# A state-space scan with a routed convolution: delta, B and C from one product, B and C spread by transfers, TensorE's work placed anew over the slots

## The chip, the cores and the metric

The kernel runs on one core of a Trainium2 chip. A core has five engines with instruction queues of their own, each in order: TensorE (PE, matmuls into PSUM), VectorE (DVE), ScalarE (ACT), GpSimd (POOL) and SyncE (SP, which here only issues DMAs); ACT issues DMAs too. Engines wait for each other through semaphores. The metric is the device time of one execution in microseconds (us), lower is better.

## The reference

Sixteen images of 48 channels, 64x64, float32, taken as two layer-norm blocks with a residual each. Block 0 ends in a feed-forward net, block 1 in another; between them stands a Mamba scan over the low frequencies of a 2-D DCT. What is computed, cut to what matters:

```python
# per image: 48 x 64 x 64, fp32
x = x + ffn0(LN(x))
w = softmax(router(LN(x)))             # a choice of experts per image
y = conv1x1(gelu(sum_e w[e] * dwconv3x3(LN(x), e)))   # routed 3x3 depthwise convolution
f = dct2(x * similarity_mask(x))       # 64 x 64 -> four quadrants q of 32 x 32, L = 1024 steps
for q in range(4):
    xi, z = in_proj[q](f[q])           # 96 channels each
    xi = silu(conv1d(xi))              # taps folded into the input product here
    dt, B, C = xp[q](xi)               # B and C: 16 states (NS) each
    delta = softplus(dt_w[q] @ dt + bias)
    h[d, n, t] = exp(delta[d, t] * A[d, n]) * h[d, n, t-1] + delta[d, t] * xi[d, t] * B[n, t]
    yq = (sum_n C[n, t] * h[d, n, t] + D[d] * xi[d, t]) * silu(z)
    f[q] = out_proj[q](yq)
x = x + y + idct2(f)
x = x + ffn1(LN(x))
```

## The kernel before

Two images are on the chip at a time, 48 channels of each in partitions 0 to 95: a **pair**. Eight pairs follow one another. Within a pair come the layer norms and the first feed-forward net, the DCT (turns and products), the **scan stage**, the inverse DCT and the second net. The routed convolution of a pair is worked off inside the scan stage of the pair before it, so the last pair's scan stage has none.

The scan stage has 8 **units** (4 quadrants x 2 images, unit v is quadrant v // 2 of image v % 2), and a unit has G = 12 **slots**. A slot holds 8 of a unit's 96 channels times 16 states = 128 partitions, over 1,024 steps. So there are 96 slots in a pair. In slot m of unit v:

- PE's `broadcast_u` (L777, L779) spreads the rows of delta*xi of slot m+1 over 128 partitions into PSUM, once DVE's scan of slot m-1 has left the bank (semaphore `h_ready`);
- ACT's `decay` (L1148) makes exp(A*delta) of slot m+2 from rows of delta that SP's `spread_delta` (L422) has fetched from DRAM (`dl`), spread over 128 partitions;
- DVE multiplies the spread rows by B, `bmat` (L1454), and runs the scan (L1459);
- POOL multiplies the states by C, `cmat` (L1542); PE's `states` (L798) sums three slots' products, and `project` (L807) is the output product of a quadrant.

Beside this, each unit prepares the next one (`prep`, `early`): `project_in` (L680) gives xi, `gate_in` (L687) z; `of_xi` (L693) multiplies xi by `wdt_all` for delta, and by `xp_rep` for B and for C. `xp_rep` is the weights of B and C with each of the 16 rows repeated 8 times, so these products already come out spread over 128 partitions; ACT copies them to `bmat` and `cmat` (`keep_b`, `keep_c`: L1074, L1082). ACT's `silu_xi`, `silu_z`, `softplus` (L1065) each need a table loaded and the table of exp loaded back (L900). `delta_to_rows` (L1088) writes delta to DRAM, `move_u` (L1094) moves rows of u. `conv` issues the taps of the convolution (L845) as matmuls of a diagonal with a shifted image, by `CONV_TAPS` in slots 5 to 9, and the 1x1 product (L851) in slot 11.

The order is written out by hand. `scan_stage` calls, for each engine, for every unit v and slot m: `early(m, v + 1)`, `step(v, m)`, `conv(m, v)`, `prep(m, v + 1)`. Tables of slots say where each part goes:

```python
PE_XI, PE_Z = 0, 2
PE_DT, PE_B, PE_C, PE_OUT = 3, (5, 6), (7, 8), (9, 10)
ACT_DT, ACT_B, ACT_C, ACT_OUT = 4, (6, 7), (8, 9), (10, 11)
CONV_TAPS = {5: (0, 1), 6: (2, 3), 7: (4,), 8: (5, 6), 9: (7, 8)}
SP_STORE, SP_LOAD = 3, 8
```

Unit 0 of a pair has nothing ahead of it: PE's `prep_first` makes its xi, delta, B and z before the first slot, and its C comes right after the first `broadcast_u`.

## Time and profile before

| | |
|---|---|
| three runs | 4363.33, 4352.52, 4356.41 us; median 4356.41 |
| the profiled execution | 4345.36 us, span 4343.6 us |
| mean granted clock of TensorE | 0.946 |
| busy share of the span | PE 90%, DVE 78%, ACT 67%, POOL 55% |
| HBM traffic | 467 MB read, 71 MB written |

The profile is of one execution. A busy share is the time in which an engine ran instructions, over the whole span; stages with different limits are mixed in it, so a stage must be looked at by itself. In the rows below the number in square brackets behind an instruction is how long its engine had stood idle, and what ended that. L-numbers are lines of the kernel before.

### The profile page before, as it was taken

The numbers are of one execution on the slowest core, as the hardware profiler recorded it, in microseconds if no ns is written. First come the engines' busy times: TensorE is split into PE (matmuls) and PEld (weight loads), VectorE is DVE, ScalarE is ACT, GpSimd is POOL, SyncE is SP. The second block draws the span as 40 slices with busy tenths as digits, with TensorE's granted clock in tenths as the row PEclk, the third lists the DMA queues.
The fourth block names the chain that finished last, engine by engine and source line by source line (L and its number), as shares of the span: only waits on it lengthen the run. The fifth ranks groups of instructions, "written<-read, shape, count | busy, mean of one in ns | idle before, by whom it ended". The sixth has DMA issues, their size and how long they took to land.

```text
span 4343.6 us, 42054 instructions
## 1 busy us (share of the span) xinstructions
PE 3908.0 (90%) x14264; PEld 1434.9 (33%) x14264; DVE 3399.8 (78%) x2997; ACT 2899.0 (67%) x3476; POOL 2381.1 (55%) x1108
## 2 busy tenths in 40 slices
PE   6889987999879998799987999889998899878987
PEld 2332234322342224422244222432234322342223
DVE  1469977699768996599965998669977699767996
ACT  2567757677576776767666775767757777576664
POOL 0138752578416874177732787238752477425774
PEclk9989999899999999899998999989989899998888
DMA  1147751677417773367624775357742576506661
GB/s 41 45 122 189 177 141 45 163 179 186 108 53 182 188 175 87 85 179 181 169 61 118 181 186 131 88 123 184 182 123 63 135 193 172 130 18 168 158 176 48
DMA packets 166830, 578.92 MB, mean 133 GB/s; under 512 B 22572, under 2 KB 23416, under 8 KB 163064
## 3 DMA queue, kind: packets, MB, share of 16 engines
q1 hardware_dynamic: 152280, 538.47, 50.4%
q10 hardware_dynamic: 14336, 37.76, 2.9%
q8 instruction: 115, 1.88, 0.2%
q14 instruction: 99, 0.81, 0.1%
HBM read 466.93 MB, written 71.48 MB: 124 GB/s over the span
## 4 chain that ended last, share of the span: by engine, by line
PE 61%; DVE 18%; ACT 11%; issue 7%; DMA 2%; POOL 0%; SPq 0%; DVEq 0%; POOLq 0%; ACTq 0%
PE ps L777 14%; PE ps L845 9%; PE ps L798 8%; DVE arena L1459 7%; PE ps L693 6%; DVE ps L1454 5%; PE ps L680 5%; PE ps L551 3%; PE ps L790 3%; PE ps L687 3%; PE ps L611 2%; ACT arena L943 2%; ACT arena L925 2%; PE ps L602 2%; PE ps L630 1%
## 5 line engine op out<-in xcount | busy, mean ns | idle before, releaser
L1542 POOL TENSOR_TENSOR arena<-arena 128x1024 f32<-128x1024 f32 x768 | 1803.8, 2358 | 842.0 <-DVE arena L1459 842.0
L1459 DVE TENSOR_TENSOR_SCAN arena<-arena,ps 128x1024 f32<-128x1024 f32 x768 | 1756.3, 2287 | 36.6 <-ACT arena L1148 10.2
L1454 DVE TENSOR_TENSOR ps<-ps,arena 128x1024 f32<-128x1024 f32 x768 | 932.4, 1214 | 178.7 <-PE ps L779 177.5
L1148 ACT ACTIVATE arena<-arena,a_all 128x1024 f32<-128x1024 f32 x768 | 865.9, 1141 | 307.3 <-DVE arena L1459 227.8
L777 PE MATMUL ps<-arena,spread 32*128 32x512 f32 x1536 | 896.6, 665 | 97.1 <-DVE arena L1459 97.1
L779 PE MATMUL ps<-arena,spread 32*128 32x512 f32 x1536 | 896.7, 665 | 0.0
L798 PE MATMUL ps<-arena,gather 128*32 128x512 f32 x3072 | 529.9, 640 | 7.0 <-POOL arena L1542 7.0
L845 PE MATMUL ps<-x 96*96 96x512 f32 x1008 | 504.5, 618 | 0.0
L777 PEld LDWEIGHTS ps<-arena,spread 32*128 32x128 f32 x1536 | 233.1, 189 | 736.9 <-issue 454.1
L1505 POOL TENSOR_TENSOR x<-x,arena 96x512 f32<-96x512 f32 x64 | 113.9, 1780 | 370.2 <-DVE arena L1324 370.2
L900 ACT ACT_TABLE_LOAD x226 | 290.0, 1283 | 23.7 <-DMA wo<-in_wo 19.6
L680 PE MATMUL ps<-arena,w_in 96*96 96x512 f32 x512 | 261.2, 657 | 36.3 <-DMA arena<-xq 36.3
L1082 ACT ACTIVATE arena<-ps 128x512 f32<-128x512 f32 x128 | 75.4, 595 | 284.1 <-PE ps L693 284.1
L693 PE MATMUL ps<-arena,xp_rep 96*128 96x512 f32 x512 | 262.4, 599 | 0.7 <-ACT arena L1074 0.7
L845 PEld LDWEIGHTS ps<-x 96*96 96x96 f32 x1008 | 142.3, 163 | 341.8 <-issue 341.8
L551 PE MATMUL ps<-arena,average 96*96 96x512 f32 x400 | 220.8, 634 | 30.6 <-ACT arena L936 30.2
L779 PEld LDWEIGHTS ps<-arena,spread 32*128 32x128 f32 x1536 | 233.1, 189 | 0.0
L798 PEld LDWEIGHTS ps<-arena,gather 128*32 128x32 f32 x3072 | 106.2, 113 | 382.5 <-issue 310.5
L925 ACT ACTIVATE arena<-ps,eps 96x512 f32<-96x512 f32 x200 | 136.4, 682 | 142.0 <-PE ps L551 142.0
L1522 POOL MEMSET arena<- 96x6 f32 x8 | 0.8, 102 | 393.3 <-ACT xq L1029 393.3
L1293 DVE TENSOR_TENSOR arena<-ps,arena 96x512 fp8e5<-96x512 f32 x128 | 86.9, 679 | 130.2 <-ACT arena L930 130.2
L943 ACT ACTIVATE arena<-ps 128x1536 f16<-128x1536 f32 x128 | 183.6, 1434 | 1.6 <-PE ps L570 1.6
(152 smaller groups left out, 5081.9 us busy)
## 6 DMA issues: line engine op xcount, KB each, us to landing
arena<-dl SPq DMA_DIRECT2D x768, 512.0 KB, 5.3
dl<-arena ACTq DMA_DIRECT2D x64, 384.0 KB, 5.9
x<-pn SPq DMA_DIRECT2D x56, 247.5 KB, 6.9
arena<-in_x SPq DMA_DIRECT2D x9, 1536.0 KB, 16.6
arena<-xq SPq DMA_DIRECT2D x64, 192.0 KB, 6.0
arena<-arena ACTq DMA_DIRECT2D x64, 192.0 KB, 5.1
...
```

Source lines behind the costliest of these rows:

```text
L551: pe.matmul(ps[0:R, LN_DEPTH + j % LN_DEPTH, :], average[:], sq[:, j % LN_DEPTH, :], start=True, stop=True).then_inc(averaged, 1)
L680: mm = pe.matmul(ps[0:DI, 6 + c, :], w_in[:, q, j, :], xs[:, i, c * 512 + 2 * j:c * 512 + 2 * j + 512], start=(j == 0), stop=(j == 1))
L693: return pe.matmul(ps[0:rows, bank, :], weights, xi[:, i, c * 512:(c + 1) * 512], start=True, stop=True)
L777: pe.matmul(ps[:, bank, :], spread[rows[0], r, :], u[rows[0], i, 0:512], start=True, stop=True)
L779: pe.matmul(ps[:, bank + 1, :], spread[rows[1], r, :], u_low[rows[1], i, :], start=True, stop=True).then_inc(ubc_ready, 1)
L798: mm = pe.matmul(ps[b * BLK:(b + 1) * BLK, c, :], gather[:, r, :], hs[:, (r * TRIO + b) % HSS, c * 512:(c + 1) * 512], start=False, stop=( ...
L845: mm = pe.matmul(ps[0:R, 7, :], diag[:, k, :], taps_of(win[:, v % 2], k), start=(k == 0), stop=(k == TAPS - 1), skip_group_check=True)
L900: exp_table = lambda: act.preload_act_table_set("natural_log_exp_and_others")
L1148: act.activation(da[:, m % DAS, :], dbc[:, m % DBC, :], ACT.Exp, scale=a_all[:, v // 2, m:m + 1]).then_inc(da_ready, 1)
L1454: dve.tensor_tensor(driven, driven, bmat[:, v % 2, :], ALU.mult).then_inc(bu_ready, 1)
L1459: dve.tensor_tensor_scan(hs[:, m % HSS, :], da[:, m % DAS, :], driven, 0.0, ALU.mult, ALU.add).then_inc(h_ready, 1)
L1542: pool.tensor_tensor(product, product, cmat[:, v % 2, :], ALU.mult).then_inc(pr_ready, 1)
```

## The change

- Delta, B and C of a unit come from one product with 128 columns, `w_dbc` (96 for delta, 16 for B, 16 for C), in PE's slot 3. ACT copies the 32 rows of B and C (`keep_bc`, one copy of 32x1024) behind `softplus` and the load of exp's table, in slot 4. Two transfers of ACT's queue, now both in slot 4, write delta (was slot 6) and the 32 rows to DRAM.
- SP spreads B and C from there: two transfers a unit (`spread_b` in slot 8, `spread_c` in slot 9), each of 16 rows repeated 8 times, 512 KB. `load_window` moves from SP's slot 8 to 10. The four `xp_rep` products and the four copies of each unit fall away.
- Unit 0 keeps the products by `xp_rep`: B ahead of the first slot as before, C behind the second `broadcast_u` instead of the first (`states_first`), and its `skip` goes from slot 3 to slot 1.
- `project_in` is split: its first half goes to slot 11 of the unit before, its second half stays in slot 0. `PE_OUT` moves from (9, 10) to (6, 8), `ACT_OUT` from (10, 11) to (7, 9).
- `keep_warm` is new: matmuls whose result nothing reads, 4 at the start of `prep_first` and 2 behind unit 0's C.
- The first convolution taps (slot 5), `project` and `project_in` wait for `bc_ready`, which is `keep_bc`'s end, instead of for `delta_ready` or `c_ready`. Slot 0 of a unit waits on DVE for B's transfer and on POOL for C's.

```diff
-PE_DT, PE_B, PE_C, PE_OUT = 3, (5, 6), (7, 8), (9, 10)
-ACT_SILU, ACT_DL, ACT_U = 1, 6, 8
-ACT_DT, ACT_B, ACT_C, ACT_OUT = 4, (6, 7), (8, 9), (10, 11)
+PE_DBC, PE_OUT, PE_XI_EARLY = 3, (6, 8), 11
+ACT_SILU, ACT_ROWS, ACT_U = 1, 4, 8
+ACT_DBC, ACT_OUT = 4, (7, 9)
 POOL_U = 5
 SP_SHIFT = 5
+SP_B, SP_C = 8, 9
 ACT_Y, POOL_GATE, S_SKIP, ACT_SILU_Z = 2, 1, 3, 3
+S_SKIP_FIRST = 1
+WARM_XI, WARM_SCAN = 4, 2
 CONV_TAPS = {5: (0, 1), 6: (2, 3), 7: (4,), 8: (5, 6), 9: (7, 8)}
 ACT_GELU, PE_PW, ACT_PW, POOL_MIX = 10, 11, 0, 1
-SP_STORE, SP_LOAD = 3, 8
...
+SP_STORE, SP_LOAD = 3, 10
...
+        delta_bc = cut(128, L)
+        delta, bc = delta_bc[0:DI], delta_bc[DI:128]
...
+                def spread_state(v, k, dst, landed, freed):
+                    sync.wait_ge(bc_out, bc_count(p, v) * 16)
+                    if v >= 2:
+                        settled(sync)
+                        sync.wait_ge(freed, (p * UNITS + v - 1) * G)
+                    rows = slice(DI + k * NS, DI + (k + 1) * NS)
+                    sync.dma_start(dst[:, v % 2, :],
+                                   a["dl"][v % 2][rows, :].rearrange("(n o) t -> n o t", o=1)
+                                   .broadcast_to([NS, DG, L])).then_inc(landed[v % 2], 16)
...
+                def keep_warm(count):
+                    for _ in range(count):
+                        pe.matmul(ps[DI:128, 0, :], gather[:, 0, :], spread[:].rearrange("p r m -> p (r m)"),
+                                  start=True, stop=True, skip_group_check=True)
                 def prep_first():
                     V = p * UNITS
+                    keep_warm(WARM_XI)
                     pe.wait_ge(xs_in[0], (p * QUADS + 1) * XSL)
                     for c in range(2):
                         project_in(V, 0, 0, c)
...
-                def first():
-                    broadcast_u(0, 0)
+                def states_first():
                     for c in range(2):
-                        of_xi(128, c, xp_rep[:, 0, 1, :], 0, c).then_inc(c_ps, 1)
+                        pe.wait_ge(xi_ready, 2 * (p * UNITS + 1) + c + 1)
+                        of_xi(128, 6 + c, xp_rep[:, 1, :], 0, c).then_inc(first_c_ps, 1)
+                    keep_warm(WARM_SCAN)
...
-                        pe.wait_ge(xs_in[i], (p * QUADS + q + 1) * XSL)
-                        pe.wait_ge(c_ready, 2 * V)
-                        if v >= 4 and i == 0:
-                            pe.wait_ge(mo_copied, 2 * (p * QUADS + q - 1))
-                        for c in range(2):
-                            if c and v >= 2 and not last:
-                                pe.wait_ge(pwb_ready, (p + 1) * NCH + v - 1)
-                            project_in(V, q, i, c)
+                        if not last:
+                            pe.wait_ge(pwb_ready, (p + 1) * NCH + v - 1)
+                        pe.wait_ge(bc_ready, bc_count(p, v - 1))
+                        project_in(V, q, i, 1)
+                    if slot == PE_XI_EARLY and v + 1 < UNITS:
+                        pe.wait_ge(xs_in[1 - i], (p * QUADS + (v + 1) // 2 + 1) * XSL)
+                        pe.wait_ge(bc_ready, bc_count(p, v))
+                        if v >= 3 and i == 1:
+                            pe.wait_ge(mo_copied, 2 * (p * QUADS + (v - 1) // 2))
+                        project_in(V + 1, (v + 1) // 2, 1 - i, 0)
                     if slot == PE_Z:
                         for c in range(2):
                             pe.wait_ge(xi_ready, 2 * V + c + 1)
+                            if v == 1:
+                                pe.wait_ge(first_c, 2 * p + c + 1)
                             gate_in(q, i, c, 6 + c)
-                    if slot == PE_DT:
+                    if slot == PE_DBC:
                         for c in range(2):
                             pe.wait_ge(sz_ready, 2 * V + c + 1)
-                            of_xi(DI, 6 + c, wdt_all[:, q, :], i, c).then_inc(dt_ready, 1)
-                    if slot in PE_B:
-                        c = PE_B.index(slot)
-                        if c == 0:
-                            pe.wait_ge(delta_ready, 2 * V + 1)
-                        else:
-                            pe.wait_ge(b_ready, 2 * V + 1)
-                        of_xi(128, 6, xp_rep[:, q, 0, :], i, c).then_inc(b_ps, 1)
-                    if slot in PE_C:
-                        c = PE_C.index(slot)
-                        if c == 0:
-                            pe.wait_ge(b_ready, 2 * V + 2)
-                        else:
-                            pe.wait_ge(c_ready, 2 * V + 1)
-                        of_xi(128, 6, xp_rep[:, q, 1, :], i, c).then_inc(c_ps, 1)
+                            of_xi(128, 6 + c, w_dbc[:, q, :], i, c).then_inc(dt_ready, 1)
...
+                    if v == 0 and m == 0:
+                        states_first()
+                    if m == (S_SKIP if v else S_SKIP_FIRST):
...
-                                pe.wait_ge(delta_ready, 2 * (p * UNITS + v + 2))
+                                pe.wait_ge(bc_ready, bc_count(p, v + 1))
...
+                def keep_bc(v):
+                    act.wait_ge(dt_ready, 2 * (p * UNITS + v) + 2)
+                    if bc_count(p, v) > 1:
+                        act.wait_ge(bc_out, (bc_count(p, v) - 1) * 16)
+                    act.activation(bc, two(6)[DI:128], ACT.Copy).then_inc(bc_ready, 1)
...
+                def bc_to_rows(v):
+                    act.wait_ge(bc_ready, bc_count(p, v))
+                    act.dma_start(a["dl"][v % 2][DI:128], bc).then_inc(bc_out, 16)
...
-                    if slot == ACT_DL:
+                    if slot == ACT_ROWS:
                         delta_to_rows(v)
+                        bc_to_rows(v)
...
+                    if m == 0 and v:
+                        dve.wait_ge(b_in[v % 2], state_in(p, v))
+                    elif m == 0:
+                        dve.wait_ge(first_b, 2 * p + 2)
```

TensorE's queue in unit 0, slots 0 to 4, as the kernel before has it (`L777`/`L779` is `broadcast_u`, `L693` with `xp_rep` is C's product, with `wdt_all` delta's, `L687` `gate_in`, `L790` `skip`):

```order
L777 MATMUL ps<-arena,spread 128x512 [waits sz_ready,u_low_in0,u_ready]
L779 MATMUL ps<-arena,spread 128x512
L693 MATMUL ps<-arena,xp_rep 128x512 x2
L777 MATMUL ps<-arena,spread 128x512 [waits b_ready]
L779 MATMUL ps<-arena,spread 128x512
L777 MATMUL ps<-arena,spread 128x512 [waits h_ready]
L779 MATMUL ps<-arena,spread 128x512
L777 MATMUL ps<-arena,spread 128x512 [waits h_ready]
L779 MATMUL ps<-arena,spread 128x512
L687 MATMUL ps<-arena,w_in 96x512 [waits xi_ready] x2
```

The same place in the changed kernel (`L811`/`L813` is `broadcast_u`, `L730` `of_xi`, `L736` `keep_warm`, `L822` `skip`, `L724` `gate_in`):

```order
L811 MATMUL ps<-arena,spread 128x512 [waits sz_ready,u_low_in0,u_ready]
L813 MATMUL ps<-arena,spread 128x512
L811 MATMUL ps<-arena,spread 128x512 [waits first_b]
L813 MATMUL ps<-arena,spread 128x512
L730 MATMUL ps<-arena,xp_rep 128x512 [waits xi_ready] x2
L736 MATMUL ps<-spread,gather 32x512 x2
L811 MATMUL ps<-arena,spread 128x512 [waits h_ready]
L813 MATMUL ps<-arena,spread 128x512
L822 MATMUL ps<-arena,dskip 96x512 x2
L811 MATMUL ps<-arena,spread 128x512 [waits h_ready]
L813 MATMUL ps<-arena,spread 128x512
L724 MATMUL ps<-arena,w_in 96x512 [waits first_c,xi_ready] x2
```

Where two broadcasts followed each other with a wait between, C's product, two fillers and the skip now stand between them.

TensorE's queue in unit 1, from `states` in slot 4 to slot 6, before (`L798` is `states`, `L845` a convolution tap):

```order
L798 MATMUL ps<-arena,gather 32x512 x5
L777 MATMUL ps<-arena,spread 128x512 [waits h_ready]
L779 MATMUL ps<-arena,spread 128x512
L845 MATMUL ps<-x 96x512 [waits delta_ready,conv_in1]
L845 MATMUL ps<-x 96x512
L693 MATMUL ps<-arena,xp_rep 128x512 [waits delta_ready]
L777 MATMUL ps<-arena,spread 128x512 [waits h_ready]
L779 MATMUL ps<-arena,spread 128x512
L845 MATMUL ps<-x 96x512 x2
L693 MATMUL ps<-arena,xp_rep 128x512 [waits b_ready]
```

And in the changed kernel (`L830` is `states`, `L879` a tap):

```order
L830 MATMUL ps<-arena,gather 32x512 x5
L811 MATMUL ps<-arena,spread 128x512 [waits h_ready]
L813 MATMUL ps<-arena,spread 128x512
L879 MATMUL ps<-x 96x512 [waits bc_ready,conv_in1]
L879 MATMUL ps<-x 96x512
L811 MATMUL ps<-arena,spread 128x512 [waits h_ready]
L813 MATMUL ps<-arena,spread 128x512
L879 MATMUL ps<-x 96x512 x2
```

The products by `xp_rep` are gone, and the taps of slot 5 wait for `bc_ready` in place of `delta_ready`.

ScalarE's queue in slot 4 of unit 1, before (`L1065` is `softplus`, `L900` the load of exp's table, `L1148` `decay`, `L1074` `keep_b`, `L1088` the transfer of delta):

```order
L1059 ACT_TABLE_LOAD
L1065 ACTIVATE arena<-ps,small_all 96x512 [waits dt_ready,delta_out,u_ready]
L1065 ACTIVATE arena<-ps,small_all 96x512 [waits dt_ready]
L900 ACT_TABLE_LOAD
L1148 ACTIVATE arena<-arena,a_all 128x1024 [waits h_ready,dbc_in0]
L1148 ACTIVATE arena<-arena,a_all 128x1024 [waits h_ready,dbc_in1]
L1074 ACTIVATE arena<-ps 128x512 [waits bu_ready,b_ps]
L1148 ACTIVATE arena<-arena,a_all 128x1024 [waits h_ready,dbc_in2]
L1088 DMA dl<-arena 96x1024 [waits delta_ready]
```

And in the changed kernel (`L1099` is `softplus`, `L934` the load of exp's table, `L1112` `keep_bc`, `L1181` `decay`, `L1118` and `L1123` the two transfers):

```order
L1093 ACT_TABLE_LOAD
L1099 ACTIVATE arena<-ps,small_all 96x512 [waits dt_ready,delta_out,u_ready]
L1099 ACTIVATE arena<-ps,small_all 96x512 [waits dt_ready]
L934 ACT_TABLE_LOAD
L1112 ACTIVATE arena<-ps 32x1024 [waits bc_out,dt_ready]
L1181 ACTIVATE arena<-arena,a_all 128x1024 [waits h_ready,dbc_in0]
L1118 DMA dl<-arena 96x1024 [waits delta_ready]
L1123 DMA dl<-arena 32x1024 [waits bc_ready]
L1181 ACTIVATE arena<-arena,a_all 128x1024 [waits h_ready,dbc_in1]
```

`keep_bc` stands between the load of exp's table and slot 4's decay, and delta's transfer has gone two slots forward.

## Rows read from the trace of the kernel before

**Rows 1.** The page: busy time, share and instructions by engine.

```profile
PE 3908.0 (90%) x14264; PEld 1434.9 (33%) x14264; DVE 3399.8 (78%) x2997; ACT 2899.0 (67%) x3476; POOL 2381.1 (55%) x1108
```

**Rows 2.** A group of the page: busy us, mean ns | idle before, releaser.

```profile
L1454 DVE TENSOR_TENSOR ps<-ps,arena 128x1024 f32<-128x1024 f32 x768 | 932.4, 1214 | 178.7 <-PE ps L779 177.5
```

**Rows 3.** Windows: stretch, us, busy PE PEld DVE ACT POOL, PEclk, DMA share, GB/s.

```profile
786.00:836.27 50.27, 45.90 (x128) 13.00 (x127) 41.44 (x24) 30.54 (x32) 28.12 (x12) 0.83 0.78 186
836.27:1095.91 259.64, 258.77 (x887) 75.95 (x888) 247.81 (x146) 193.54 (x204) 204.28 (x91) 1.00 0.74 182
1095.91:1137.77 41.86, 36.20 (x118) 9.17 (x117) 41.13 (x24) 16.80 (x16) 31.34 (x14) 0.88 0.42 105
3926.00:4272.98 346.98, 301.46 (x972) 79.02 (x971) 328.98 (x192) 212.11 (x220) 255.22 (x109) 0.86 0.64 163
```

**Rows 4.** Timeline of VectorE in unit 3: start, us, instruction.

```profile
939.64 1.21 DVE L1454 TENSOR_TENSOR ps<-ps,arena 128x1024 f32<-128x1024 f32 x1
...
943.08 1.21 DVE L1454 TENSOR_TENSOR ps<-ps,arena 128x1024 f32<-128x1024 f32 x1
944.32 2.29 DVE L1459 TENSOR_TENSOR_SCAN arena<-arena,ps 128x1024 f32<-128x1024 f32 x1
```

**Rows 5.** Timeline of TensorE in the same unit.

```profile
939.46 1.92 PE L798 MATMUL ps<-arena,gather 128*32 128x512 f32 x12
941.30 0.69 PE L777 MATMUL ps<-arena,spread 32*128 32x512 f32 x1
...
942.36 1.96 PE L845 MATMUL ps<-x 96*96 96x512 f32 x4
944.16 1.02 PE L693 MATMUL ps<-arena,xp_rep 96*128 96x512 f32 x2
945.11 0.69 PE L777 MATMUL ps<-arena,spread 32*128 32x512 f32 x1
```

**Rows 6.** Timeline of TensorE as pair 1's scan stage starts.

```profile
770.71 5.37 PE L680 MATMUL ps<-arena,w_in 96*96 96x512 f32 x8 [4.64 <-DMA arena<-xq]
...
791.06 0.69 PE L777 MATMUL ps<-arena,spread 32*128 32x512 f32 x1 [2.21 <-DVE arena L1459]
```

**Rows 7.** Timeline of VectorE in pair 1's unit 0; windows there.

```profile
788.72 2.29 DVE L1459 TENSOR_TENSOR_SCAN arena<-arena,ps 128x1024 f32<-128x1024 f32 x1 [1.49 <-ACT arena L1148]
...
810.30 1.23 DVE L1454 TENSOR_TENSOR ps<-ps,arena 128x1024 f32<-128x1024 f32 x1 [4.46 <-PE ps L779]
...
791.90:809.00 17.10, 14.97 (x22) 4.06 (x20) 12.86 (x8) 10.23 (x10) 11.00 (x5) 0.50 0.80 188
```

**Rows 8.** L1454 in the last pair: VectorE's idle time before it, and times.

```profile
  PE ps L779: 18.9, 7
```

**Rows 9.** Timeline of ScalarE in unit 3.

```profile
931.06 1.02 ACT L1172 ACTIVATE arena<-ps 96x1024 f32<-96x1024 f32 x1
...
940.67 1.28 ACT L900 ACT_TABLE_LOAD   x1
941.96 2.19 ACT L1148 ACTIVATE arena<-arena,a_all 128x1024 f32<-128x1024 f32 x2
```

**Rows 10.** Timeline of TensorE: pair 1's last unit, then the last pair.

```profile
1099.50 1.22 PE L777 MATMUL ps<-arena,spread 32*128 32x512 f32 x1 [1.64 <-DVE arena L1459]
...
3965.87 0.86 PE L777 MATMUL ps<-arena,spread 32*128 32x512 f32 x1 [1.54 <-DVE arena L1459]
```

**Rows 11.** Windows: behind each of these waits; pair 5's last unit, and in it.

```profile
1099.10:1105.90 6.80, 6.40 (x18) 1.58 (x20) 6.73 (x5) 1.84 (x2) 4.71 (x2) 0.50 0.78 180
3966.30:3969.70 3.40, 3.40 (x13) 0.58 (x12) 3.37 (x3) 1.10 (x2) 2.31 (x2) 0.50 0.99 234
3183.03:3233.93 50.90, 46.32 (x118) 10.97 (x117) 41.44 (x24) 16.90 (x16) 31.25 (x14) 0.70 0.35 87
3194.90:3222.20 27.30, 27.30 (x54) 6.05 (x52) 19.37 (x11) 7.28 (x7) 16.62 (x8) 0.50 0.41 104
```

**Rows 12.** The page's DMA issues: KB, us to landing.

```profile
arena<-dl SPq DMA_DIRECT2D x768, 512.0 KB, 5.3
```

More of the change, by code:

```diff
@@ L110, in program @@
         small_all = sb("small_all", [DI, QUADS, WS])
-        wdt_all = sb("wdt_all", [DI, QUADS, DI])
-        xp_rep = sb("xp_rep", [DI, QUADS, 2, 128])
+        w_dbc = sb("w_dbc", [DI, QUADS, DI + 2 * NS])
+        xp_rep = sb("xp_rep", [DI, 2, 128])
         w_in = sb("w_in", [R, QUADS, 3, DI])
@@ L186, in program @@
         cmat = two_of(cut(128, 2 * L))
-        delta = cut(DI, L)
+        delta_bc = cut(128, L)
+        delta, bc = delta_bc[0:DI], delta_bc[DI:128]
         u = two_of(cut(DI, 2 * L))
@@ L263, in program @@
         dt_ready = sem("dt_ready")
-        b_ps = sem("b_ps")
-        c_ps = sem("c_ps")
-        b_ready = sem("b_ready")
-        c_ready = sem("c_ready")
+        first_b_ps = sem("first_b_ps")
+        first_c_ps = sem("first_c_ps")
+        first_b = sem("first_b")
+        first_c = sem("first_c")
+        bc_ready = sem("bc_ready")
+        bc_out = sem("bc_out")
+        b_in = [sem("b_in0"), sem("b_in1")]
+        c_in = [sem("c_in0"), sem("c_in1")]
         delta_ready = sem("delta_ready")
@@ L291, in program @@
             (dt_w, "dt_w"), (a_log, "a_log"), (small_all[:], "small"),
-            (xp_rep[:], "xp_rep"), (wi_raw, "wi_raw"), (cw, "conv_bc"), (wo[:], "wo"),
+            (w_dbc[:, :, DI:], "xp_bc"), (xp_rep[:], "xp_rep"), (wi_raw, "wi_raw"), (cw, "conv_bc"), (wo[:], "wo"),
         ]
@@ L444, in prep @@
                         shifted(v + 1)
+                    if v and slot == SP_B:
+                        spread_b(v)
+                    if v and slot == SP_C:
+                        spread_c(v)
                 def first():
@@ L870, in final @@
                     project(QUADS - 1, 1, 7)
-                scan_stage(prep, first, step, conv, final)
+                scan_stage(prep, lambda: broadcast_u(0, 0), step, conv, final)
                 pe.wait_ge(mo_copied, (p + 1) * 2 * QUADS)
@@ L1104, in early @@
                         exp_table()
-                    if slot == ACT_DT:
+                    if slot == ACT_DBC:
                         softplus(v)
                         exp_table()
-                    if slot in ACT_B:
-                        keep_b(v, ACT_B.index(slot), 6)
-                    if slot in ACT_C:
-                        keep_c(v, ACT_C.index(slot), 6)
+                        keep_bc(v)
                 def prep_first():
@@ L1537, in step @@
                     n = V * G + m
-                    if m == 0:
-                        pool.wait_ge(c_ready, 2 * V + 2)
+                    if m == 0 and v:
+                        pool.wait_ge(c_in[v % 2], state_in(p, v))
+                    elif m == 0:
+                        pool.wait_ge(first_c, 2 * p + 2)
                     pool.wait_ge(h_ready, n + 1)
@@ L1673, in layouts @@
     o["wo"] = wo
-    o["xp_rep"] = np.repeat(xp[:, rank:].reshape(QUADS, 2, NS, DI), DG, axis=2).transpose(3, 0, 1, 2)
+    o["xp_bc"] = xp[:, rank:].transpose(2, 0, 1)
+    o["xp_rep"] = np.repeat(xp[0, rank:].reshape(2, NS, DI), DG, axis=1).transpose(2, 0, 1)
     o["xp_dt"] = xp[:, 0:rank].transpose(1, 0, 2)
```

46 lines of the change are left out of this document (20 added, 26 removed).

## The prediction, before the changed kernel ran

> **What bounds the kernel now.** On the page TensorE is busy 90% of the span, VectorE 78% [rows 1]. The mean hides stages, so I took VectorE's multiply next: it stood idle 178.7 us in all, 177.5 of it for `broadcast_u` [rows 2]. Then the windows of one pair's scan stage [rows 3]. VectorE's slots follow each other every 943.08 - 939.64 = 3.44 us (3.45 below) when nothing is late [rows 4], so a unit costs at least 12 x 3.45 = 41.4. [...] Unit 7, which prepares nothing, takes 41.86 [rows 3]. [...] The last pair takes 346.98 at a mean clock of 0.86 [rows 3], and VectorE waits 18.9 for broadcasts in it [rows 8].
>
> **The change, part by part**, on this pair and times seven.
>
> 1. Products. A product of B or C costs 945.11 - 944.16 = 0.95 [rows 5]. Four leave each unit, 3.8 us, out of slots 5 to 8. The delta product goes from 96 to 128 columns at the same 512 rows; the `xp_rep` products have 128 columns already, so I cost it alike. Nothing is added on TensorE but fillers. Slot 5 had broadcast 1.06 (942.36 - 941.30), taps 1.80, product 0.95 [rows 5]: 3.81, over 3.45. After: 2.86. The whole unit held 258.77 / 6 = 43.1 [rows 3] and then holds 39.3 of 41.4. Slots 3, 7 and 11, and in even units 6 and 8 with `project` (about 1), still hold more than 3.45, each beside slots under 3. So units 1 to 6 fall to VectorE's pace: 6 x 41.4 = 248.4, plus 0.4 in each of three even units where `project` now stands ahead of slot 7, 249.6. Gain 10.0 a pair, **70**. Unit 7 already runs there.
>
> 2. Unit 0. The C product, two fillers and the skip fill the place of the 2.21 wait. I take all of VectorE's waits there as gone but the first scan's: 41.4 + 1.5 = 42.9 against 50.27, 7.4 a pair, **52**. If the clock falls there all the same, this is 0.
>
> 3. Last pair. 346.98 against 8 x 41.4 + 1.5 = 332.7. Its TensorE idles more, not less, as it has no convolution; but without the four products and with `project_in` halved, each slot has more than half its time free, so even at half clock few broadcasts are late. I leave 2.3 for those: 335, **12**. Bounds 0 and 14.
>
> 4. Fillers. Four ahead of `project_in` lie in TensorE's idle time of 4.64 that a DMA ends [rows 6]. No row shows a filler (32 rows of output, 512 columns). Each lies between a sixth of a `states` group of 1.84 and a product's 0.95 [rows 5], 1.2 to 3.8 in all against 4.64 at full clock, twice that at half. I take 0.5 us late per pair, 8 x 0.5 = **4 lost**; below, a gain of up to 1.5 a pair, if they keep the clock of the 5.37 us project_in up; above, 3 lost.
>
> 5. ScalarE. Four copies go, one of 32x1024 comes, no table with it. The nearest row is a copy of 96x1024 out of PSUM, 1.02 [rows 9]; as low bound 0.35 by partitions. It stands between exp's table load (ends 941.96) and the decays (941.96, two in 2.19) [rows 9]: so it ends at 943.0, slot 4's decay, which slot 6's scan needs, at 944.05, and that scan started at 944.32 [rows 4]. It fits, by 0.27. If the copy took 1.5 and this is on the path in all 48 units, it would cost 11.
>
> 6. Transfers. B and C as two of 512 KB a unit, like the twelve of delta, which land in 5.3 [rows 12]. They are issued in slots 8 and 9 and wanted at slots 12 and 12.5: 13 us for 5.3. Two in some 15 more raise the DMA share from 0.74 [rows 3] to about 0.84; the delta transfers behind them on SP's queue get two issues ahead of them, and have slots of lead. Cost 0; each 1 us late would cost 42.
>
> 7. The taps of slot 5 now wait for `keep_bc`'s end. This is the part that I price highest. TensorE's broadcast in slot 5 ended at 942.36 [rows 5] when it was behind; unhindered, it ends about 941.5. The taps may start at 943.05. So a wait of 1.5 us arises in each of six units of seven pairs, **42 waits**, where before TensorE had none. By itself it costs nothing: taps to 944.85, broadcast to 945.9, and slot 7 needs it at 946.5. But the rows show what such a wait did to the clock. A wait of 1.64 ahead of the last unit stood in all seven pairs that have one, and each time the clock fell to 0.50; in pair 1 for 6.8 us [rows 10, 11], with broadcasts of 1.22 in place of 0.69. In the last pair 1.54 was enough, for a fall of 3.4 us [rows 10, 11]. In such a fall TensorE loses 1.7 of work, in one of 6.8 us 3.4. Against this stand margins of 0.6 at slot 7 and 0.8 at slot 9 in odd units, and -0.1 and -0.5 in even ones, which also hold `project` (0.4 of that is counted). So a fall costs 1.1 or 2.7 in odd units, 1.8 or 3.5 in even ones: mean 2.3. I take 2.2, for a few units that keep the clock: 42 x 2.2 = **92 lost**.
>
> [...]
>
> **Sum.** -70 - 52 - 12 + 4 + 92 = -38. The profiled execution was 4345.4; the runs' median is 11 above it, so against the median 4356 - 38 = **4318**.
>
> **Rivals.**
>
> *The clock holds.* The wait of 1.5 is a hair under the 1.54 that was followed by a fall, and it could be shorter: `keep_bc` at 0.35 makes it 0.9. Unit 7's 1.64 wait always brought it down, which speaks against. Then the 92 are not lost: 4356 - 130 = 4226. If it is found only in odd units or at some phases, between the two.
>
> *The clock falls and stays down (slower).* In pair 5's last unit it was at 0.50 for 27.3 us, at first with small gaps between; the unit took 50.90 against 41.86 [rows 3, 11], 9.0 lost in one fall. [...] With 4.5 a unit, half of that 9.0, 42 units lose 189: +59, 4415. It decides from 130 / 42 = 3.1 us lost a unit.
>
> *ScalarE or the DMAs take the bound.* `keep_bc` waits also for the end of the former transfer and could take its decays past due by 1 to 2 us in 48 units, or C's transfer lands late under a share of 0.84. With 1 us a unit and the falls of the clock: 4318 + 42 = 4360, no change. Speaks against it: 0.27 free by the longest nearby copy, 13 us against 5.3.
>
> *The gain in unit 0 fails.* Fillers don't hold the clock: 4318 + 52 = 4370. Against: the new order leaves no wait over 1 us there. I count it with the last rival.
>
> **How the numbers follow.** Forecast 0.45, clock holds 0.22, stays down 0.24, others 0.09. The forecast's own range is 42 x (1.1 to 3.1): 4272 to 4356. A measurement tells some 0.3% (13 us) from no change. Faster by more: 0.22 + 0.36 of the forecast's 0.45 + 0.03 = 0.61; slower: 0.20 + 0.03 = 0.23; the rest 0.16. The range from 4215 to 4400 leaves out the far end of "stays down" and a clock that holds with more gain than counted, together 0.2.
>
> **What would show it.** In the changed profile: units 1 to 6 near 41.6 where the clock is 1.00, over 43 where it is lower; on TensorE a wait of about 1.5 ahead of the taps in slot 5, released by ScalarE; a mean clock in windows of units 1 to 6 under 0.95 (forecast), 1.00 (clock holds), under 0.8 (stays down). Unit 0 near 43 with no wait over 1 us on TensorE. The last pair near 335. The idle time before VectorE's multiply released by a DMA would show the transfers late; before the scan released by ScalarE, `keep_bc`. The prediction is wrong if that wait ahead of the taps is under 1 us or the clock pays no heed to it, or if a fall lasts longer than 6.8 us.

## The result and the profile after

The changed kernel takes 4505.35 us (median of 4 runs, 4501.25 to 4527.41) against 4355.64 for the kernel before: a ratio of 1.0348, 95% interval 1.032 to 1.0376. It is slower by 150 us where I forecast 38 us less.

From the page of the kernel after, in the order of the sections: busy time by engine, the granted clock in 40 slices, groups (busy us, mean ns | idle before, releaser) and DMA issues (count, KB, us to landing).

```profile
PE 3951.2 (88%) x13912; PEld 1396.9 (31%) x13912; DVE 3398.7 (76%) x2997; ACT 2847.9 (63%) x3308; POOL 2380.2 (53%) x1108
...
PEclk9988889998999989989898888998999888898888
...
L1181 ACT ACTIVATE arena<-arena,a_all 128x1024 f32<-128x1024 f32 x768 | 866.8, 1143 | 779.6 <-DMA arena<-dl 444.0
L1489 DVE TENSOR_TENSOR ps<-ps,arena 128x1024 f32<-128x1024 f32 x768 | 932.1, 1214 | 327.9 <-PE ps L813 327.6
...
L879 PE MATMUL ps<-x 96*96 96x512 f32 x1008 | 567.6, 686 | 47.2 <-ACT arena L1112 47.1
L717 PE MATMUL ps<-arena,w_in 96*96 96x512 f32 x512 | 266.4, 651 | 60.3 <-ACT x L1221 60.3
...
arena<-dl SPq DMA_DIRECT2D x880, 512.0 KB, 6.6
```

TensorE has 352 fewer matmuls and yet is busy 43 us longer than in [rows 1]. VectorE's wait for `broadcast_u` has grown from 177.5 [rows 2] to 327.6, by 150 of the 158 us between the two profiled executions: that is where the loss is spent. Two waits of TensorE are new: 47.1 ahead of the convolution taps, released by `keep_bc` (L1112), and 60.3 ahead of `project_in` (L717), released by `mix_bias` (L1221). ScalarE's decays wait 444.0 for the transfers of delta. The 512 KB transfers, the new ones of B and C among them, take 6.6 us to land in place of 5.3 [rows 12].

Windows of the kernel after (stretch, us, busy PE, PEld, DVE, ACT, POOL, granted clock, DMA share, GB/s): pair 0's units 0 and 1, a stretch within unit 1, units 1, 2 and 3 of pair 3, then the scan stages of pair 0 and of the last pair.

```profile
263.59:312.12 48.53, 44.46 (x124) 11.82 (x123) 41.28 (x24) 29.50 (x29) 28.15 (x12) 0.86 0.91 215
312.12:359.70 47.58, 45.55 (x137) 12.24 (x136) 41.25 (x25) 30.60 (x30) 33.96 (x15) 0.86 0.74 192
333.40:347.10 13.70, 13.70 (x28) 2.99 (x26) 9.71 (x6) 4.84 (x5) 8.88 (x4) 0.50 1.00 276
1953.06:1997.71 44.65, 40.98 (x134) 11.10 (x133) 41.25 (x25) 29.45 (x29) 33.94 (x15) 0.92 0.81 193
1997.71:2046.98 49.27, 45.38 (x146) 12.40 (x145) 41.54 (x25) 33.85 (x33) 33.96 (x15) 0.90 0.80 196
2046.98:2089.22 42.24, 38.80 (x137) 10.94 (x136) 41.15 (x25) 29.16 (x29) 34.00 (x15) 1.00 0.81 207
263.59:648.78 385.19, 363.49 (x1078) 95.62 (x1076) 330.38 (x192) 233.96 (x230) 263.59 (x116) 0.85 0.73 180
4096.54:4431.57 335.03, 276.53 (x918) 69.92 (x916) 328.09 (x192) 204.79 (x199) 255.38 (x109) 0.84 0.81 193
```

Of the units shown, the one at clock 1.00 takes 42.24, under the 43.3 of [rows 3]. The others are at 0.86 to 0.92 and take 44.6 to 49.3. The last pair, which has no convolution, takes 335.0 against 347.0.

TensorE's timeline in unit 1 of pair 0, and VectorE's behind it:

```profile
330.16 0.69 PE L811 MATMUL ps<-arena,spread 32*128 32x512 f32 x1
...
332.84 3.20 PE L879 MATMUL ps<-x 96*96 96x512 f32 x4 [1.55 <-ACT arena L1112]
335.97 1.22 PE L811 MATMUL ps<-arena,spread 32*128 32x512 f32 x1
...
347.14 1.10 PE L879 MATMUL ps<-x 96*96 96x512 f32 x2
348.17 0.69 PE L811 MATMUL ps<-arena,spread 32*128 32x512 f32 x1
```

```profile
338.10 1.23 DVE L1489 TENSOR_TENSOR ps<-ps,arena 128x1024 f32<-128x1024 f32 x1 [1.77 <-PE ps L813]
...
343.76 1.23 DVE L1489 TENSOR_TENSOR ps<-ps,arena 128x1024 f32<-128x1024 f32 x1 [2.11 <-PE ps L813]
...
349.34 1.23 DVE L1489 TENSOR_TENSOR ps<-ps,arena 128x1024 f32<-128x1024 f32 x1 [2.03 <-PE ps L813]
```

The wait that I had priced is there, 1.55 long. Behind it the clock is at 0.50 for 13.7 us (the third window), in which TensorE is busy for all of the 13.70, and VectorE waits in three slots, 5.9 us, the last of them just behind the stretch.

In pair 3 the wait stands elsewhere. ScalarE's and then TensorE's timeline as its unit 2 starts:

```profile
2002.22 1.15 ACT L1181 ACTIVATE arena<-arena,a_all 128x1024 f32<-128x1024 f32 x1 [3.25 <-DMA arena<-dl]
2003.27 0.67 ACT L1221 ACTIVATE x<-ps,pw_bias 96x512 f32<-96x512 f32 x1
```

```profile
2003.99 3.73 PE L717 MATMUL ps<-arena,w_in 96*96 96x512 f32 x4 [3.33 <-ACT x L1221]
2007.65 1.22 PE L811 MATMUL ps<-arena,spread 32*128 32x512 f32 x1
```

A decay waits 3.25 for its transfer, `mix_bias` stands behind it in ScalarE's queue, and the second half of `project_in` waits for `mix_bias`. Then the clock is down there too, at 0.50 from 2003.99 to 2007.65: this second half takes 3.73, where the first half, six us before and at 1.00, took 1.88.

Not every such wait had a fall behind it. In units 3 and 5 of this pair TensorE waits 1.54 and 1.68 for `mix_bias` and 1.03 and 1.01 ahead of the taps, and the clock is 1.00 throughout; they take 42.2 and 42.4.

### The profile page after: what moved, and what is told of

It reads as the page before. It is cut to its first block, busy times and chain, and to the rows that moved or that the text cites. A ratio compares the mean times of both kernels' runs of the same rounds, so it can differ in the third digit from the quotient of the medians.

```text
span 4501.1 us, 41464 instructions
## 1 busy us (share of the span) xinstructions
PE 3951.2 (88%) x13912; PEld 1396.9 (31%) x13912; DVE 3398.7 (76%) x2997; ACT 2847.9 (63%) x3308; POOL 2380.2 (53%) x1108
## 4 chain that ended last, share of the span: by engine, by line
PE 30%; DVE 25%; ACT 19%; issue 15%; DMA 5%; POOL 5%; SPq 0%; DVEq 0%; POOLq 0%; ACTq 0%
DVE arena L1494 10%; DVE ps L1489 9%; PE ps L879 6%; PE ps L811 5%; DMA arena<-dl 5%; PE ps L830 4%; PE ps L588 3%; POOL arena L1579 3%; POOL arena L1588 2%; PE ps L648 2%; ACT arena L977 2%; ACT arena L1181 2%; ACT arena L959 2%; ACT L934 2%; PE ps L639 2%
## 5 line engine op out<-in xcount | busy, mean ns | idle before, releaser
L1494 DVE TENSOR_TENSOR_SCAN arena<-arena,ps 128x1024 f32<-128x1024 f32 x768 | 1756.3, 2287 | 38.3 <-ACT arena L1181 10.7
L1181 ACT ACTIVATE arena<-arena,a_all 128x1024 f32<-128x1024 f32 x768 | 866.8, 1143 | 779.6 <-DMA arena<-dl 444.0
L1489 DVE TENSOR_TENSOR ps<-ps,arena 128x1024 f32<-128x1024 f32 x768 | 932.1, 1214 | 327.9 <-PE ps L813 327.6
L811 PE MATMUL ps<-arena,spread 32*128 32x512 f32 x1536 | 955.7, 705 | 102.6 <-DVE arena L1494 95.7
L813 PE MATMUL ps<-arena,spread 32*128 32x512 f32 x1536 | 948.7, 706 | 0.0
L830 PE MATMUL ps<-arena,gather 128*32 128x512 f32 x3072 | 605.2, 719 | 5.3 <-POOL arena L1579 5.3
L879 PE MATMUL ps<-x 96*96 96x512 f32 x1008 | 567.6, 686 | 47.2 <-ACT arena L1112 47.1
L811 PEld LDWEIGHTS ps<-arena,spread 32*128 32x128 f32 x1536 | 247.9, 200 | 811.6 <-issue 509.4
L717 PE MATMUL ps<-arena,w_in 96*96 96x512 f32 x512 | 266.4, 651 | 60.3 <-ACT x L1221 60.3
L1540 POOL TENSOR_TENSOR x<-x,arena 96x512 f32<-96x512 f32 x64 | 113.9, 1780 | 371.9 <-DVE arena L1357 371.9
L879 PEld LDWEIGHTS ps<-x 96*96 96x96 f32 x1008 | 154.9, 177 | 438.5 <-issue 438.5
L830 PEld LDWEIGHTS ps<-arena,gather 128*32 128x32 f32 x3072 | 115.1, 123 | 456.3 <-issue 406.5
L813 PEld LDWEIGHTS ps<-arena,spread 32*128 32x128 f32 x1536 | 244.7, 200 | 0.0
L1588 POOL TENSOR_TENSOR arena<-arena 96x1024 f32<-96x1024 f32 x64 | 150.8, 2356 | 147.7 <-ACT arena L1205 147.7
L1540 POOL TENSOR_TENSOR x<-col_all,arena 96x512 f32<-96x512 f32 x64 | 104.8, 1638 | 141.0 <-DVE arena L1357 141.0
```

The lines of the kernel that those rows point to most:

```text
L717: mm = pe.matmul(ps[0:DI, 6 + c, :], w_in[:, q, j, :], xs[:, i, c * 512 + 2 * j:c * 512 + 2 * j + 512], start=(j == 0), stop=(j == 1))
L811: pe.matmul(ps[:, bank, :], spread[rows[0], r, :], u[rows[0], i, 0:512], start=True, stop=True)
L813: pe.matmul(ps[:, bank + 1, :], spread[rows[1], r, :], u_low[rows[1], i, :], start=True, stop=True).then_inc(ubc_ready, 1)
L830: mm = pe.matmul(ps[b * BLK:(b + 1) * BLK, c, :], gather[:, r, :], hs[:, (r * TRIO + b) % HSS, c * 512:(c + 1) * 512], start=False, stop=( ...
L879: mm = pe.matmul(ps[0:R, 7, :], diag[:, k, :], taps_of(win[:, v % 2], k), start=(k == 0), stop=(k == TAPS - 1), skip_group_check=True)
L1181: act.activation(da[:, m % DAS, :], dbc[:, m % DBC, :], ACT.Exp, scale=a_all[:, v // 2, m:m + 1]).then_inc(da_ready, 1)
```

## The experiments

Two theories at first. **A**: the wait ahead of the taps in slot 5 brings the clock down, and that is the loss. **B**: the two added transfers a unit make decays late at the unit's end, the lateness passes through ScalarE's queue to TensorE, and that wait brings the clock down. The versions named a to k below all start from the changed kernel but c3 and d4, which start from the kernel before.

**a1: the copy ahead of the table.**

```diff
                         softplus(v)
-                        exp_table()
                         keep_bc(v)
+                        exp_table()
```

> The changed kernel with the copy of B and C's rows ahead of the load of exp's table, not behind it: the taps of slot 5 may start 1.3 us sooner, the decays at the same time as before. Theory A (the wait of up to 1.55 us ahead of the taps is what brings the clock down): nearly all of the loss goes, 4240 us or less, granted clock over 0.96. Theory B (crowded transfers in slots 8 to 10 make decays late, ScalarE's queue late, and the second half of project_in wait for it, and that wait brings the clock down): little, 4450 to 4500. If both act in different pairs: some 4400, with units that kept the 1.55 us wait down from 47.6 to about 45.

**a2: tiny spreads.** All waits stay, but B and C are not brought in: the products with them use what lies in the buffers.

```diff
-                    sync.dma_start(dst[:, v % 2, :],
-                                   a["dl"][v % 2][rows, :].rearrange("(n o) t -> n o t", o=1)
-                                   .broadcast_to([NS, DG, L])).then_inc(landed[v % 2], 16)
+                    sync.dma_start(dst[0:NS, v % 2, 0:64],
+                                   a["dl"][v % 2][rows, 0:64]).then_inc(landed[v % 2], 16)
```

> The changed kernel with each spread of B and C cut to 16 rows of 64 numbers (the products with B and C then use what lies in the buffers; all waits stay). Theory A: no change, 4490 to 4505, the waits of 1.55 us are in every unit. Theory B: decays no longer wait for transfers, no wait of 3 us ahead of the second half of project_in, 4330 to 4400. If both act: waits of 1.55 us ahead of the taps in all 42 units and falls behind them, 4400 to 4480.

**a3: both edits.**

> Both edits in one (the output is again made from what lies in the buffers). Theories A and B together leave nothing else to lose: about 4226 us (4210 to 4250), units 1 to 6 at 41.4 to 41.8, granted clock 1.00 in them. If it stays over 4300, a third cause is open, such as TensorE's own idle gaps between slots that now hold less work.

Measured: a1 4488.06 (ratio 1.0298, interval 1.0252 to 1.0343), a2 4508.57 (1.0334, 1.0292 to 1.0375), a3 4218.63 (0.9683, 0.9651 to 0.9714). Either edit alone gives back nearly nothing; together they give back 287 us. Neither theory alone stood: each of the two waits by itself is enough to lose nearly all of it. The rows of waits (engine and line, released by, us in total, times, longest) show it, from a1, then from a2:

```profile
ACT arena L1181 <- DMA arena<-dl: 665.3, 379, 4.8
...
PE ps L717 <- ACT x L1221: 113.9, 41, 4.0
```

```profile
ACT arena L1180 <- DMA arena<-dl: 211.0, 121, 4.5
...
PE ps L878 <- ACT arena L1111: 73.3, 46, 2.0
```

In a1 the wait ahead of the taps is all but gone (2.5 in all, the longest 0.7), and the wait for `mix_bias` has doubled, from 60.3 to 113.9: units that are no longer held back at slot 5 run into the late transfers. In a2 it is the other way round, with 73.3 ahead of the taps, nearly all in waits of 1.55.

a2 also shows what a fall costs, since a wait at one and the same place (1.55 to 1.57 long in all but one of units 1 to 6, 1.69 to 1.99 in unit 0) was followed by a fall 39 times and by none 7 times. Windows of its pair 4, units 4, 5 and 6, and the wait in the first two:

```profile
2663.39:2712.46 49.07, 47.03 (x144) 12.38 (x143) 41.37 (x26) 32.23 (x32) 33.98 (x15) 0.86 0.67 165
2712.46:2753.80 41.34, 39.73 (x139) 11.39 (x138) 40.92 (x25) 30.61 (x30) 33.98 (x15) 1.00 0.79 193
2753.80:2796.32 42.52, 40.13 (x142) 10.81 (x140) 41.26 (x25) 32.49 (x32) 34.01 (x15) 1.00 0.78 185
```

```profile
2684.12 2.70 PE L878 MATMUL ps<-x 96*96 96x512 f32 x4 [1.56 <-ACT arena L1111]
...
2733.19 1.93 PE L878 MATMUL ps<-x 96*96 96x512 f32 x4 [1.56 <-ACT arena L1111]
```

With the wait and no fall an odd unit takes 41.3 and an even one 42.5. With the wait and a fall, of 10.2 to 17.1 us, odd units take 45.9 to 47.6 and even ones 49.1 to 51.0. The wait itself costs nothing in odd units and 1.2 in even ones (a unit of a3, below, takes 41.3); the fall, in which the granted clock is 0.50, costs 4.6 to 8.5.

Windows of a3, pair 1: unit 0, units 1 to 6, the whole scan stage:

```profile
776.08:818.78 42.70, 38.47 (x125) 10.79 (x124) 40.94 (x24) 29.42 (x29) 28.18 (x12) 1.00 0.93 221
818.78:1066.86 248.08, 239.32 (x838) 67.04 (x836) 245.58 (x145) 189.44 (x186) 204.00 (x90) 1.00 0.79 194
776.08:1108.46 332.38, 312.73 (x1078) 86.60 (x1076) 327.69 (x192) 234.98 (x230) 263.87 (x116) 0.98 0.76 187
```

With both waits cut short (the longest left are 0.7 ahead of the taps and 1.3 for `mix_bias`) unit 0 takes 42.7 and units 1 to 6 take 248.1, at clock 1.00: VectorE's pace. TensorE is idle for 8.8 of the 248 us, in pieces of which the longest is 0.91, and the clock does not fall there. The decays wait 341.3 for their transfers in a3 too, without the traffic of B and C and without a loss.

**a4: no fillers** (`WARM_XI, WARM_SCAN = 0, 0`).

> The changed kernel without its six filler matmuls a pair. If they hold the clock in unit 0, unit 0 grows from 44 to 48 up to 50, and the time by 20 to 40 us. If they do nothing, the same time within 5 us; if they only delay the first product, 4 us less.

Measured: 4503.53 (1.0317, 1.0274 to 1.0359), no change in the time. Unit 0 took 48.4 to 48.6 in each of the first seven pairs, against 44.0 to 48.8 with fillers, but the units behind it were no slower in those pairs. So the time doesn't tell what they are worth here. Its last pair took 366.5, with a fall of 37.5 us in it.

**c1: the window in slot 5**, on top of a1 (`SP_STORE, SP_LOAD = 3, 5`).

> The copy of B and C's rows ahead of the table (as in a1), and the load of the convolution's window in SP's slot 5 instead of 10, away from the two spreads. Theory B (it is the crowd of transfers in slots 8 to 10 that makes the first decays of the next unit late): decays wait less than the 665 us of a1, no wait of 3 us ahead of project_in's second half, 4225 to 4280 us. Rival (the two spreads alone are enough to crowd it): as a1, 4460 to 4500.

**c2: mix_bias ahead of the decay**, on top of a1 (called in `early` of slot 0, and in `conv` for the last unit only).

```diff
                 def early(slot, v):
+                    if slot == ACT_PW and v >= 2 and not last:
+                        mix_bias(v - 2)
```

> As a1, and ScalarE's mix_bias stands ahead of the decay in slot 0 instead of behind it; the transfers are as crowded as in a1. If the chain is late transfer, decay, mix_bias, second half of project_in, clock: the decays still wait some 600 us for transfers, but TensorE's wait of 3 us is gone and the time is 4225 to 4290. If late transfers hurt in another way too (a scan that waits for its decay, the first broadcast that waits for move_u), it stays over 4350.

**c4: all three.**

> The changed kernel with all three moves: copy ahead of the table, window load in slot 5, mix_bias ahead of the decay. If the two waits on TensorE were all that the change lost: 4215 to 4235 us, as the run with both edits of the transfers' size, with the right output, and faster than before by 3%. If c1 or c2 alone is enough, no faster than that one.

Measured: c1 4349.55 (0.9975, 0.9957 to 0.9992), c2 4341.83 (0.9968, 0.9940 to 0.9997), c4 4341.45 (0.9966, 0.9940 to 0.9991). Each takes some 140 us off a1 and ends 0.2 to 0.4% under before, and both together are no better. In c2 the decays still waited 659.7 for transfers: it is the path through `mix_bias` to TensorE that costs, not their lateness as such. But all missed what was expected of them, by 50 to 106 us: something else is then late. In c4 the first broadcast of a unit waited 24 times, 50.1 us in all, for `move_u` to land; behind 11 of these waits a fall began within 2.3 us, behind 13 none. And in the profiles of c2 and c4 the last pair, which neither of the two waits touches, took 353 in place of 335, with a fall of 30.7 us in it: by the profiles some 18 us of the miss lie there.

**c3: the wait alone, in the kernel before.**

```diff
-                                pe.wait_ge(delta_ready, 2 * (p * UNITS + v + 2))
+                                pe.wait_ge(da_ready, (p * UNITS + v) * G + 7)
```

> The kernel before, with one wait changed: the first taps of slot 5 wait for the decay of slot 4, which ends when the changed kernel's copy of B and C would. TensorE, which is the bound there, gets a wait of about 0.7 us in seven units of seven pairs. If a wait there costs only its own length: 49 x 0.7 = 34, 4390 us. If it brings the clock down as in the changed kernel (about 3 to 6 us a unit): 4500 to 4650.

Measured: 4529.08 (1.0390, 1.0355 to 1.0424), 171 us slower by one wait. From c3's waits, and a unit of pair 1 in which the clock kept up:

```profile
PE ps L845 <- ACT arena L1148: 54.3, 42, 1.8
```

```profile
870.37:914.47 44.10, 42.33 (x144) 12.47 (x144) 41.40 (x26) 31.53 (x33) 34.04 (x15) 1.00 0.76 180
```

The waits themselves sum to 54.3. The unit shown has a wait of 1.51 and no fall, and takes 44.1 where the kernel before takes 42.5: it loses the wait's own length. Of 28 waits of 1.5 in units 1 to 6, 13 were of this kind; 14 waits of 0.83 never had a fall behind them. Most of the rest of the loss is in the 15 others: 14 units of 51.7 to 53.7 at a mean clock of 0.84 to 0.87, one of 46.8 at 0.96. That wait ahead of the taps is enough for the loss with the products, the copies and the transfers as they were before, but not with a fall behind it each time.

**d1: move_u a slot earlier**, on top of c4 (`ACT_U` from 8 to 7).

> The version with all three moves (c4), and move_u, whose landing the first broadcast of a unit waits for, issued in ScalarE's slot 7 instead of 8. In c4 that broadcast waited 24 times, 50.1 us in all, for it, and the clock was low behind it. If this wait is the one left: it goes, and the time is 4215 to 4250. If the crowd of transfers only shifts the lateness elsewhere: 4320 to 4345 as c4.

**d2: d1 without fillers.**

> As d1, without the six filler matmuls a pair. In the changed kernel without fillers unit 0 took 48.4 to 48.6 in each pair, against 42 to 44 in most with them. If that is their worth once nothing else holds the clock down: 35 to 50 us more than d1. If not: the same within 10.

**d3: rows first**, on top of d1 (`bc_to_rows` right behind `keep_bc`, ahead of the table; `SP_B, SP_C = 7, 9`).

> As d1, and the rows of B and C are written ahead of delta's, right behind their copy, and B is spread in slot 7 instead of 8: the transfers lie further apart. If crowding of slots 8 and 9 still costs in d1: 10 to 60 us under d1. If SP's queue now waits for the rows to land and holds the delta transfers up: over d1.

Measured: d1 4369.89 (1.0023, 0.9997 to 1.0049), d2 4352.42 (0.9991, 0.9966 to 1.0017), d3 4355.16 (0.9990, 0.9963 to 1.0018). d1 missed: the wait for `move_u` was gone, and in its place TensorE waited ahead of the 1x1 product of slot 11, for `gelu`, which stands behind a late decay in ScalarE's slot 10. From d1's waits:

```profile
ACT arena L1183 <- DMA arena<-dl: 598.4, 295, 5.6
...
PE ps L885 <- ACT arena L1234: 52.2, 33, 2.9
```

In d2 unit 0 took 48.0 to 48.5 in every pair, against 42.3 to 44.2 in d1, and the time was no longer than d1's; with the later units scattering between 41.3 and 50 that difference is lost. Spreading the transfers out (d3) came out 15 us under d1, at the near end of what was expected, but the intervals overlap: it tells little.

**d4: unit 0's part alone, in the kernel before**: fillers, C's product behind the second broadcast, skip in slot 1.

```diff
+                    if v == 0 and m == 0:
+                        states_first()
+                    if m == (S_SKIP if v else 1):
-                    if m == S_SKIP:
                         skip(v)
```

> The kernel before with the part of the change that concerns unit 0 alone: six fillers a pair, C's product behind the second broadcast, skip in slot 1; all products as before. My second term, 7.4 us in each of seven pairs and some 7 in the last, says 4290 to 4310. If unit 0's gain only came with the lighter slots of the rest: 4330 to 4360.

Measured: 4305.00 (0.9887, 0.9863 to 0.9910), as expected. Windows of its pair 1, unit 0 and units 1 to 6:

```profile
785.65:828.45 42.80, 40.79 (x130) 11.52 (x128) 41.06 (x24) 30.47 (x32) 28.14 (x12) 1.00 0.93 217
828.45:1088.00 259.55, 258.74 (x887) 76.02 (x888) 247.74 (x145) 193.27 (x204) 204.27 (x91) 1.00 0.72 182
```

Unit 0 falls from 50.27 [rows 3] to 42.80, the rest is as it was. (Fillers and order were changed together here; a4 and d2 are the runs without fillers.) A filler is to be seen too (x4 is two of them; 1.90 us, 0.95 each):

```profile
788.24 1.90 PE L699 MATMUL ps<-spread,gather 128*32 128x512 f32 x4
790.38 0.69 PE L791 MATMUL ps<-arena,spread 32*128 32x512 f32 x1 [0.24 <-DVE arena L1473]
```

**f1: tiny C**, on top of d1 (C's spread cut as in a2, B's whole).

> As d1 (copy ahead of the table, window load in slot 5, mix_bias ahead of the decay, move_u a slot earlier), with the spread of C cut to 16 rows of 64 numbers and the spread of B whole. If the traffic of two more 512 KB transfers a unit is what makes the decays late in d1 (waits of 598 us for transfers), one of them less brings most of the remaining 130 us back: 4220 to 4290. If already one is too much, it stays at 4330 to 4370.

**f2: gelu ahead of the decay** in slot 10, on top of d1.

```diff
+                    if m == ACT_GELU and not last:
+                        gelu(v)
                     if w < UNITS:
                         decay(w, k)
```

> As d1, all transfers whole, and ScalarE's gelu stands ahead of the decay in slot 10 instead of behind it. In d1 TensorE waited 33 times, 52.2 us in all, for that gelu ahead of the 1x1 product in slot 11. If this is the last such wait: 4215 to 4260. If late transfers reach TensorE in yet another way, as they did each time before: 4300 to 4360.

**h1: C by transfer, B by products**, on top of c4.

```diff
-                    if v and slot == SP_B:
-                        spread_b(v)
+                    if slot in PE_B:
+                        of_xi(128, 6, xp_rep[:, q, 0, :], i, c).then_inc(b_ps, 1)
```

> Half of the change: C by a transfer, B by the two products by xp_rep and two copies as before (slots 5 and 6; output product in slots 8 and 9), on top of c4's three moves. TensorE then has 41.2 us of work in a slot sequence of 41.4, so no gaps of its own, and one transfer less crowds the DMAs. If idle gaps and late transfers are all that the change loses: 4230 to 4280, below before and below the version with unit 0's part alone (4305). If TensorE's fuller slots bring back waits in single slots: 4290 to 4330.

**k1: h1 with f2's and d1's moves.**

> h1 (C by transfer, B by products) with f2's moves as well: gelu ahead of the decay in slot 10, move_u in slot 7. If the late decays still cost something in h1 through TensorE's waits: 4235 to 4250. If h1 has nothing left to lose there but VectorE's 0.8 us in three units and what TensorE's fuller slots cost: the same as h1 within 8 us.

Measured: f1 4331.86 (0.9942, 0.9913 to 0.9972), f2 4276.24 (0.9797, 0.9769 to 0.9825), h1 4256.78 (0.9764, 0.9739 to 0.9789), k1 4266.32 (0.9795, 0.9769 to 0.9821). f1 came where its second case had it: one transfer less gave 38 us of the 130 looked for, the decays still waited 555.6 and TensorE still 46.3 for `gelu`. f2, with all the traffic, came within 16 us of its expectation's upper end: it was again the path to TensorE. h1, as expected, has the lowest median of the versions that compute the whole reference, 2.4% under before; its interval overlaps those of f2 and k1. Windows of its pair 1: unit 0, units 1 to 6, unit 7:

```profile
774.75:817.35 42.60, 40.13 (x129) 11.54 (x128) 40.94 (x24) 31.17 (x32) 28.15 (x12) 1.00 0.98 234
817.35:1069.25 251.90, 248.50 (x862) 71.48 (x860) 246.90 (x146) 195.00 (x197) 203.86 (x90) 1.00 0.80 203
1069.25:1112.38 43.13, 37.56 (x117) 9.17 (x116) 41.13 (x24) 16.22 (x15) 31.64 (x14) 0.84 0.43 102
```

TensorE is busy 248.5 of 251.9 at clock 1.00 in all six units. VectorE waits 0.4 ahead of slots 10 and 11 in units 2, 4 and 6, where `project` stands in slots 8 and 9; the six units take 3.8 more than in a3, and that is what B's products and the moved `project` cost there. k1's moves gave nothing more: 9.5 over h1, where at most 8 was expected.

## Why the prediction was wrong, step by step

**Step 1, units 1 to 6 at VectorE's pace: right, where the clock stays up.** Forecast 249.6 a pair; 248.1 in a3, and 42.24 for the unit of the changed kernel shown at clock 1.00. The gain of 10.0 a pair is against the 259.64 of [rows 3], where TensorE is busy 258.77 at clock 1.00.

**Step 2, unit 0: right in kind, its sum in part by luck.** Forecast 42.9, against 50.27 [rows 3] with the clock at 0.50 for 17.1 us of it [rows 7], and 52 us in all; d4 measured 42.8 in pair 1, at clock 1.00, and 51 in all (4355.6 - 4305.0). By the profiles unit 0 gives 44.5 in seven pairs (348.4 to 303.9), since pairs 4 and 5 had stood at 48.5 before and pair 0 stays at 47.2. Nine more come from pair 5's last unit, 50.9 before [rows 11] and 41.8 in d4, which the edit doesn't touch. In the changed kernel unit 0 took 43.9 to 48.8: in pairs 0, 4 and 6 it has a wait of 1.9 to 2.0 ahead of its taps and takes 47.0 to 48.8, in the others a wait of 1.1 to 1.6 ahead of the delta product, for `silu_z`, with a fall of 6.8 us behind it.

**Step 3, the last pair: right.** Forecast 335, measured 335.0. But it is not a steady number: the versions made from the changed kernel, whose last pair holds the same work or nearly so, show 334.3 to 353.1 (c2), and 366.5 without fillers (a4).

**Step 4, fillers: small, as said**, but each takes 0.95, at the upper end of my bounds. Unit 0 took 48.0 to 48.5 without them (d2) and 42.3 to 44.2 with them (d1). In the time that did not show.

**Step 5, ScalarE: right.** The copy takes 1.02, and the scans wait 10.7 for decays in place of 10.2.

**Step 6, transfers at a cost of 0: wrong.** I weighed 13 us of lead against 5.3 and looked only at what waits for B and C. With them the delta transfers are late (6.6 to land, decays waiting 444 to 665 in place of 77 in the kernel before; a part of it is there without their traffic, 341 in a3, where the units are short), and what stands behind a decay in ScalarE's queue is late with it: `mix_bias`, `gelu`. With the wait ahead of the taps gone (a1) this alone costs 269 us (4488.1 - 4218.6). I had named this rival at 1 us a unit; it is 269 / 42 = 6.4 if all is put on 42 units, and 5.5 by the profiles (units 1 to 6 take 1972.0 in a1 and 1740.0 in a3).

**Step 7, the wait ahead of the taps: place, length and effect right, size wrong.** 1.5 forecast, 1.55 measured. Two numbers in it failed. I priced a fall at 2.2 us a unit, from falls of 3.4 and 6.8 us, though rows of mine had longer ones, 17.1 [rows 7] and 27.3 [rows 11]. Behind this wait they lasted 13.7 or 17.1 in the changed kernel but for one of 10.2, and cost 4.6 to 8.5 each in a2; a fall longer than 6.8 us was what I had named as the sign of being wrong. With this wait as the main one (a2) the loss is 290 us (4508.6 - 4218.6). And the waits can arise in 49 units, not 42: unit 0 also prepares a unit. That is 290 / 49 = 5.9 us for each place, though the clock kept up behind 7 of a2's 46 waits. That is the step on which the forecast fell. The rival "falls and stays down" had the sign and came nearest, from the one fall of 27.3 us in [rows 11]; at 4.5 us a unit it said 4415, still 90 short, and its own sign did not show: it wanted a mean clock under 0.8 in units 1 to 6, and that is 0.88. The loss is far past the point, 3.1 a unit, from which it decides.

**The sum.** The terms but for steps 6 and 7 made 4226; a3 gives 4218.6. They do not agree one by one. By the profiles a3's scan stages gain 149 us (2814.4 to 2665.8) where the terms have 134, 10 of it in last units, which I had left alone. All that lies outside them loses 37 (1529.2 to 1565.8) where I had 4: from pair 0 to pair 1 it is 176.0 at a clock of 0.92, against 170.4 at 0.95. In part the near hit is luck. Both losses did not add: 4508.6 and 4488.1 alone, 4505.4 together. My reading, which no run tests by itself: a unit that has lost its time in slot 5 gives the transfers time to land.

The loss was a multiple of the waits themselves: c3's 54.3 us of waits cost 171. It was paid again and again, but not at every wait: a fall stood behind 15 of the 28 waits of 1.5 us in c3, and behind 39 of 46 in a2.

What stays open is which wait brings the clock down, and how long a fall lasts. TensorE was busy for all of the 13.70 us at 0.50 in the window shown, and for all of the 27.3 in [rows 11]; no run here separates what ends a fall, or what tells the 7 waits of a2 without a fall from the 39 with one. Open too is why the transfers of a1 are as late as they are; d3 moved them apart with no effect clear of noise, and f1 halved the added traffic for little, while h1, which differs from f1 in more than the traffic, has decays waiting 273.5 only.
